# A second cross attention: query weights loaded first, the first batch's scores and softmax placed among the absorbed queries

## The chip, the cores and the metric

The kernel runs on one core of a Trainium2 chip. The metric is the device time of one execution in microseconds (us).

## What is computed

The reference is a perceiver-like network on `x` (8 batches x 64 tokens x 256 features) with a context of 8 x 1024 x 256: three sublayers (cross attention, a memory mixer, a mixture feed-forward), then three more, of which the first is the cross attention that the change touches. Each is added to the residual. Cut to that sublayer:

```python
x = x + _L1_xattn_ref(_layernorm(x), ctx_1024, ctx_1024, w_q, w_k, w_v, w_o)
# HEADS = 16, HEAD_DIM = 64, scale = HEAD_DIM ** -0.5
q = (query @ w_q).reshape(B, Q, HEADS, HEAD_DIM).transpose(0, 2, 1, 3)
k = (key @ w_k).reshape(B, Kl, HEADS, HEAD_DIM).transpose(0, 2, 1, 3)
v = (value @ w_v).reshape(B, Kl, HEADS, HEAD_DIM).transpose(0, 2, 1, 3)
scores = jnp.einsum('bhqd,bhkd->bhqk', q, k) * scale
attn = jax.nn.softmax(scores, axis=-1)
out = jnp.einsum('bhqk,bhkd->bhqd', attn, v)
return out.transpose(0, 2, 1, 3).reshape(B, Q, HEADS * HEAD_DIM) @ w_o
```

## The kernel before

The program runs the sublayers one after another, each as one or more blocks of five instruction streams (TensorE, VectorE, ScalarE, GpSimd, SyncE for the loads). A block ends for all engines together; inside it, the order of each engine's work is written out by hand and the engines wait for each other's semaphores. Precise products are made of three matmuls (`product3`) on a high half (a cast to fp32r) and a low half (value minus high half): high x high, high x low, low x high.

The second cross attention (`xattn1`, from line 1285) has three blocks.

Block e (lines 1314 to 1389). SyncE loads the key weights `wk` (L1327), the query weights `wq` (L1328), the context features of batch 0 (`rawT`, feature-major, L1307) and its keys (`raw`, L1310), 1 MB each. Meanwhile `Norm` normalises the residual and transposes it into `xnT`; it opens with 12 matmuls on the identity (L100). Both weights count on one semaphore, `w_in`, and ScalarE and TensorE wait for both loads. Then:

- Query projection, 8 groups p (two heads each): TensorE runs 4 matmul passes with `wq` (L1378) into one of two PSUM banks; ScalarE casts the result to `q_hi` (L1348), VectorE makes `q_lo` (L1363). In front, ScalarE casts all of `wk` (L1345) and GpSimd subtracts (L1335).
- Absorbed queries, 32 units u = (head, half of the 256 features): three matmuls with `wk` (64 rows each) into one of four PSUM banks; even units are evicted by ScalarE with the scale (L1351), odd ones by VectorE (L1367), into `e_qc`. After unit 0, ScalarE casts the context features, in two copies, to `e_cT_hi` (L1356).

Block f (from line 1395). It starts with the queries of batch 0 split into halves of four groups each: ScalarE casts 128x1024 (`f_qb_hi`, L1462), VectorE subtracts (L1529). GpSimd subtracts the features' high half in four pieces (`e_cT_lo`, L1436). TensorE then makes the scores of group 0 and group 1 (12 matmuls of 128x512 each, `scores`), which wait for all four pieces and for the first half of the queries. The softmax of a group p is: VectorE's maximum (L1541), ScalarE's exponential with the sum (L1474), VectorE's reciprocal and multiplication (L1547, L1549). After that the eight batches run, the first and last written out and the six between as a loop. In a batch TensorE transposes the probabilities of group p (L1594), makes the scores of group p + 2 and the outputs of an earlier pair of groups; ScalarE and VectorE split the transposed probabilities (L1482, L1536) and do the softmax of p + 2. In the last two groups the next batch's first two scores and the first softmax are made, so a batch starts with group 0 softmaxed and group 1 scored. SyncE loads the features and keys of the next batch as soon as the buffers have been read.

Block g multiplies by `w_v` and `w_o` and adds to the residual.

## Time and profile before

| | us |
|---|---|
| median of 3 runs | 1137.87 (1135.56 to 1143.01) |
| time of the profiled execution | 1139.35 |
| its span (first to last instruction) | 1137.6 |
| TensorE matmul busy | 1028.3 (90%) |
| VectorE busy | 559.2 (49%) |
| ScalarE busy | 494.1 (43%) |
| GpSimd busy | 209.5 (18%) |

One execution was profiled. Times in the profile are microseconds from the start of its span. PE is TensorE's matmuls, PEld its weight loads, DVE VectorE, ACT ScalarE, POOL GpSimd, SPq SyncE's DMA queue. A row of a timeline is one instruction or several alike in a row (x2, x8), written as output <- inputs with partitions x elements; its duration is that of the whole group, and overlapping matmuls have modelled ends, so their pace is read from the starts. The granted clock is a share of 2.4 GHz.

### The profile page before, as it was taken

To read this page: it belongs to the slowest core of one execution; us is meant where nothing else is said; L and a number is where in the kernel's file an instruction comes from. 1 tells how busy PE (TensorE), PEld (TensorE's weight loads), DVE (VectorE), ACT (ScalarE), POOL (GpSimd) and SP (SyncE) were. 2 spreads that over 40 slices of the span, in tenths; PEclk is the share of its full clock that TensorE was granted. 3 is DMA by queue.
4 is the path that set the end of the run, shared out by engine and by line. 5 is a ranking of instruction groups with operands and counts; after the bars stand their busy time and mean duration, and the time that the engine had idled before them with its cause. 6 is when DMAs were issued, how large, how long until landed. Compare 5 with 4: busy or idle time off the path is not lost. (4 is left out here: it accounts for less than half of the span.)

```text
span 1137.6 us, 20074 instructions
## 1 busy us (share of the span) xinstructions
PE 1028.3 (90%) x8322; PEld 863.3 (76%) x8322; DVE 559.2 (49%) x837; ACT 494.1 (43%) x719; POOL 209.5 (18%) x173
## 2 busy tenths in 40 slices
PE   8999999745779997879999999999999988969997
PEld 6787778515458995569898989898988956459997
DVE  3556655667744343554645454555465512373211
ACT  4566665331327662634444444444544411313222
POOL 2111120020603441131111111111303003120000
PEclk9899999987969998989999999999999999889999
DMA  4111110010112314020111111111030003912710
GB/s 135 60 58 41 44 42 2 6 37 16 44 38 66 94 62 148 1 75 13 63 37 37 37 37 37 37 37 37 37 111 0 1 1 111 380 43 90 243 39 19
DMA packets 49535, 68.75 MB, mean 60 GB/s; under 512 B 5744, under 2 KB 41024, under 8 KB 49472
## 3 DMA queue, kind: packets, MB, share of 16 engines
q1 hardware_dynamic: 49472, 67.83, 18.0%
q8 instruction: 49, 0.80, 0.3%
q14 instruction: 14, 0.11, 0.0%
HBM read 67.29 MB, written 0.52 MB: 60 GB/s over the span
## 5 line engine op out<-in xcount | busy, mean ns | idle before, releaser
L1474 ACT ACTIVATE f_pr<-ps,f_negmax 128x1024 f32<-128x1024 f32 x64 | 71.4, 1116 | 178.9 <-DVE f_negmax L1541 178.9
L181 PE MATMUL ps<-f_pT_hi,f_cN_hi 128*128 128x256 f32 x512 | 145.3, 284 | 2.4 <-DVE f_pT_lo L1536 2.4
L181 PE MATMUL ps<-f_pT_hi,f_cN_lo 128*128 128x256 f32 x512 | 144.8, 283 | 0.0
L181 PE MATMUL ps<-f_pT_lo,f_cN_hi 128*128 128x256 f32 x512 | 144.8, 283 | 0.0
L1536 DVE TENSOR_TENSOR f_pT_lo<-ps,f_pT_hi 128x1024 fp32r<-128x1024 f32 x64 | 78.2, 1222 | 78.6 <-ACT f_pT_hi L1482 78.6
L378 DVE SCALAR_TENSOR_TENSOR a_u<-ps,a_floor,a_cap 128x1024 f32<-128x1024 f32 x64 | 79.2, 1279 | 75.5 <-PE ps L468 75.5
L181 PE MATMUL ps<-e_cT_hi,f_qb_hi 128*128 128x512 f32 x256 | 106.2, 415 | 8.0 <-POOL e_cT_lo L1436 8.0
L181 PEld LDWEIGHTS ps<-f_pT_hi,f_cN_hi 128*128 128x128 f32 x512 | 98.0, 191 | 4.8 <-DVE f_pT_lo L1536 2.6
L181 PE MATMUL ps<-e_cT_hi,f_qb_lo 128*128 128x512 f32 x256 | 101.1, 395 | 0.0
L181 PE MATMUL ps<-e_cT_lo,f_qb_hi 128*128 128x512 f32 x256 | 100.5, 393 | 0.0
L181 PEld LDWEIGHTS ps<-f_pT_lo,f_cN_hi 128*128 128x128 f32 x512 | 98.0, 191 | 1.6
L181 PEld LDWEIGHTS ps<-f_pT_hi,f_cN_lo 128*128 128x128 f32 x512 | 98.0, 191 | 0.0
L318 ACT ACTIVATE a_pr<-a_u,a_nb 128x1024 f32<-128x1024 f32 x64 | 73.7, 1152 | 52.0 <-DVE a_u L378 50.7
L1541 DVE TENSOR_REDUCE f_negmax<-ps 128x1 f32<-128x1024 f32 x64 | 78.1, 1220 | 36.8 <-PE ps L181 36.8
L1482 ACT CAST f_pT_hi<-ps 128x1024 fp32r<-128x1024 f32 x64 | 64.9, 1014 | 53.9 <-PE ps L1594 53.9
L1436 POOL TENSOR_TENSOR e_cT_lo<-e_rawT,e_cT_hi 128x512 fp32r<-128x512 f32 x32 | 42.3, 1357 | 220.4 <-ACT e_cT_hi L1458 193.5
L1594 PE MATMUL ps<-ident,f_pr 128*128 128x128 f32 x512 | 66.6, 273 | 12.7 <-DVE f_pT_lo L1536 11.9
L1594 PEld LDWEIGHTS ps<-ident,f_pr 128*128 128x128 f32 x512 | 57.0, 140 | 17.8 <-issue 16.4
L100 PE MATMUL ps<-ident 128*128 128x128 f32 x240 | 37.6, 329 | 35.5 <-ACT b_cs L632 18.4
L1443 POOL TENSOR_TENSOR f_cN_lo<-e_raw,f_cN_hi 128x512 fp32r<-128x512 f32 x32 | 43.7, 1396 | 120.7 <-ACT f_cN_hi L1469 120.7
L100 PEld LDWEIGHTS ps<-ident 128*128 128x128 f32 x240 | 36.2, 243 | 38.1 <-ACT b_cs L632 19.2
L181 PEld LDWEIGHTS ps<-e_cT_hi,f_qb_hi 128*128 128x128 f32 x256 | 48.7, 190 | 16.4 <-POOL e_cT_lo L1436 8.4
(360 smaller groups left out, 2201.0 us busy)
## 6 DMA issues: line engine op xcount, KB each, us to landing
k_w<-in_L_ffn_W SPq DMA_DIRECT2D x22, 1024.0 KB, 9.8
a_ctxT<-in_ctxT SPq DMA_DIRECT2D x16, 512.0 KB, 4.4
d_w<-in_L_ffn_w SPq DMA_DIRECT2D x32, 256.0 KB, 2.8
e_rawT<-in_ctxT SPq DMA_DIRECT2D x8, 1024.0 KB, 4.9
e_raw<-in_ctx SPq DMA_DIRECT2D x8, 1024.0 KB, 5.3
e_wk<-in_L_xattn_w_k SPq DMA_DIRECT2D x1, 1024.0 KB, 7.1
e_wq<-in_L_xattn_w_q SPq DMA_DIRECT2D x1, 1024.0 KB, 9.2
g_wv<-in_L_xattn_w_v SPq DMA_DIRECT2D x1, 1024.0 KB, 8.0
```

The source lines that it names most:

```text
L100: self.nc.tensor.matmul(self.bank(bank)[:, 0:P], self.ident[:], self.ident[:], start=True, stop=True)
L181: last = nc.tensor.matmul(out, a[i], b[j], start=start and n == 0, stop=stop and n == 2, skip_group_check=skip)
L318: A.activation(pr[:, n % NP, :], u[:, n % NU, :], ACT.Square, bias=nb[:], scale=HD ** -0.5).then_inc(p_ready, 1)
L378: V.scalar_tensor_tensor(u[:, n % NU, :].rearrange("p (r w) -> p r w", r=RT), core.psum[:, 0:2048].rearrange("p (r w) -> p r w", r=RT)[:, ...
L1436: nc.gpsimd.tensor_tensor(cT[1][:, c, cols], rawT[:, c, cols], cT[0][:, c, cols].bitcast(F32), ALU.subtract).then_inc(t_lo, 1)
L1443: nc.gpsimd.tensor_tensor(cN[1][:, ks, :], raw[:, ks, :], cN[0][:, ks, :].bitcast(F32), ALU.subtract).then_inc(n_lo, 1)
L1474: nc.scalar.activation(pr[:, p % NPR, :], core.ps[p % 2][:], ACT.Exp, bias=negmax[:, p:p + 1], accum_out=total[:, p:p + 1]).then_inc(exp_r ...
L1482: nc.scalar.copy(pT[0][:, g, :, P * (p % 2):P * (p % 2) + P], core.ps[2][:].rearrange("p (k n) -> p k n", n=P)).then_inc(pT_hi, 1)
L1536: nc.vector.tensor_tensor(pT[1][:, g, :, cols], core.ps[2][:].rearrange("p (k n) -> p k n", n=P), pT[0][:, g, :, cols].bitcast(F32), ALU.s ...
L1541: nc.vector.tensor_reduce(negmax[:, p:p + 1], core.ps[p % 2][:], AX, ALU.max, negate=True).then_inc(max_ready, 1)
L1594: last = nc.tensor.transpose(core.ps[2][:, k * P:(k + 1) * P], pr[:, p % NPR, k * P:(k + 1) * P], core.ident[:])
```

## The change

The query weights are loaded first and have a semaphore of their own. The key weights' high and low halves are made in two pieces, and the features' high half in two, between the casts of the query projection (ScalarE after groups 0 and 1, and after 2 and 3); the low half of the features stands behind that of the key weights in GpSimd's queue, in block e. The units are evicted as before in two halves of 16; after each half, ScalarE waits until both engines' evictions are done and casts that half of batch 0's queries, and VectorE subtracts, in front of its next eviction. After unit 22 TensorE makes the scores of group 0; VectorE takes their maximum after evicting unit 23 and divides after evicting unit 29; ScalarE takes the exponential after evicting unit 26. After unit 31 TensorE makes the scores of group 1. Block f starts with the maximum of group 1 and then the batches, whose order stays. The buffers and helpers that both blocks now use are declared in front of them. No instruction is dropped; two are split in two (the key weights' cast and subtraction).

```diff
--- before.py
+++ after.py
@@ -1298,6 +1298,14 @@
+        NPR = 2
+        HALF = HP // 2
+        qb = [core.sb("e_qb_" + n, [P, DC, H * T], F32R, ctx) for n in ("hi", "lo")]
+        pr = core.sb("e_pr", [P, NPR, S], F32, ctx)
+        negmax, total = core.sb("e_negmax", [P, HP], F32, ctx), core.sb("e_total", [P, HP], F32, ctx)
+        qb_hi, qb_lo = core.sem("e_qb_hi"), core.sem("e_qb_lo")
+        s_psum, max_ready, exp_ready = core.sem("e_s_psum"), core.sem("e_max_ready"), core.sem("e_exp_ready")
+        recip, p_ready = core.sem("e_recip"), core.sem("e_p_ready")
         norm = Norm(core, "e")
...
@@ -1309,6 +1317,59 @@
         def load_keys(sp, b):
             sp.dma_start(raw[:], one(a["ctx"], b).rearrange("(k p) d -> p k d", p=P)).then_inc(n_in, 16)
 
+
+        def queries_of(b, half):
+            cols = slice(HALF * P * half, HALF * P * (half + 1))
+            return qc[:, :, b, cols] if isinstance(b, int) else \
+                qc[:, :, bass.ds(b, 1), cols].rearrange("p c o n -> p c (o n)")
+
+        def act_queries(b, half):
+            cols = slice(HALF * P * half, HALF * P * (half + 1))
+            nc.scalar.copy(qb[0][:, :, cols], queries_of(b, half)).then_inc(qb_hi, 1)
+
+        def dve_queries(dve, b, half):
+            cols = slice(HALF * P * half, HALF * P * (half + 1))
+            dve.wait_ge(qb_hi, 2 * b + half + 1)
+            nc.vector.tensor_tensor(qb[1][:, :, cols], queries_of(b, half), qb[0][:, :, cols].bitcast(F32),
+                                    ALU.subtract).then_inc(qb_lo, 1)
+
+        def pool_features(pool, b):
+            for i in range(4):
+                c, cols = i // 2, slice(S // 2 * (i % 2), S // 2 * (i % 2 + 1))
+                pool.wait_ge(t_hi, 2 * b + c + 1)
+                nc.gpsimd.tensor_tensor(cT[1][:, c, cols], rawT[:, c, cols], cT[0][:, c, cols].bitcast(F32),
+                                        ALU.subtract).then_inc(t_lo, 1)
+
+        def act_exponentials(act, b, p):
+            act.wait_ge(max_ready, HP * b + p + 1)
+            nc.scalar.activation(pr[:, p % NPR, :], core.ps[p % 2][:], ACT.Exp, bias=negmax[:, p:p + 1],
+                                 accum_out=total[:, p:p + 1]).then_inc(exp_ready, 1)
+
+        def dve_maximum(dve, b, p):
+            dve.wait_ge(s_psum, HP * b + p + 1)
+            nc.vector.tensor_reduce(negmax[:, p:p + 1], core.ps[p % 2][:], AX, ALU.max,
+                                    negate=True).then_inc(max_ready, 1)
+
+        def dve_divide(dve, b, p):
+            n = HP * b + p
+            dve.wait_ge(exp_ready, n + 1)
+            nc.vector.reciprocal(total[:, p:p + 1], total[:, p:p + 1]).then_inc(recip, 1)
+            dve.wait_ge(recip, n + 1)
+            nc.vector.tensor_scalar(pr[:, p % NPR, :], pr[:, p % NPR, :], total[:, p:p + 1], None,
+                                    ALU.mult).then_inc(p_ready, 1)
+
+        def pe_scores(pe, b, p):
+            if p == 0:
+                pe.wait_ge(t_lo, 4 * b + 4)
+            if p % HALF == 0:
+                pe.wait_ge(qb_lo, 2 * b + p // HALF + 1)
+            wait_if_positive(pe, exp_ready, HP * b + p - 1)
+            for h in range(2):
+                for c in range(DC):
+                    last = product3(nc, core.bank(2 * (p % 2) + h),
+                                    [q[:, c, p * P:(p + 1) * P] for q in qb],
+                                    [t[:, c, 512 * h:512 * h + 512] for t in cT], c == 0, c == DC - 1)
+            last.then_inc(s_psum, 1)
 
         with ExitStack() as inner:
             sb = lambda name, shape, dt=F32: core.sb("e_" + name, shape, dt, inner)
...
@@ -1316,23 +1377,28 @@
             q2 = [sb("q_" + n, [P, HP, NT], F32R) for n in ("hi", "lo")]
-            w_in, wk_hi, wk_lo = sem("w_in"), sem("wk_hi"), sem("wk_lo")
+            wq_in, wk_in, wk_hi, wk_lo = sem("wq_in"), sem("wk_in"), sem("wk_hi"), sem("wk_lo")
             q_psum, q_hi, q_lo = sem("q_psum"), sem("q_hi"), sem("q_lo")
             c_psum, c_act, c_dve, dve_step = sem("c_psum"), sem("c_act"), sem("c_dve"), sem("dve_step")
             block = inner.enter_context(nc.Block())
             NB = 4
+            EARLY = 22
 
             @block.sync
             def _(sp):
-                sp.dma_start(wk[:], a["L1_xattn_w_k"].rearrange("(p r) d -> r p d", r=P)).then_inc(w_in, 16)
-                sp.dma_start(wq[:], a["L1_xattn_w_q"].rearrange("(c p) o -> p c o", p=P)).then_inc(w_in, 16)
+                sp.dma_start(wq[:], a["L1_xattn_w_q"].rearrange("(c p) o -> p c o", p=P)).then_inc(wq_in, 16)
+                sp.dma_start(wk[:], a["L1_xattn_w_k"].rearrange("(p r) d -> r p d", r=P)).then_inc(wk_in, 16)
                 load_features(sp, 0)
                 load_keys(sp, 0)
 
             @block.gpsimd
             def _(pool):
-                pool.wait_ge(wk_hi, 1)
-                nc.gpsimd.tensor_tensor(wk2[1][:], wk[:], wk2[0][:].bitcast(F32), ALU.subtract).then_inc(wk_lo, 1)
+                for i in range(2):
+                    pool.wait_ge(wk_hi, i + 1)
+                    ps = slice(HALF * i, HALF * (i + 1))
+                    nc.gpsimd.tensor_tensor(wk2[1][:, ps, :], wk[:, ps, :], wk2[0][:, ps, :].bitcast(F32),
+                                            ALU.subtract).then_inc(wk_lo, 1)
+                pool_features(pool, 0)
 
             def into(u):
                 h, c = u // DC, u % DC
@@ -1340,20 +1406,33 @@
 
             @block.scalar
             def _(act):
-                norm.scalar(act)
-                act.wait_ge(w_in, 32)
-                nc.scalar.copy(wk2[0][:], wk[:]).then_inc(wk_hi, 1)
-                for p in range(HP):
+                def high(p):
                     act.wait_ge(q_psum, p + 1)
                     nc.scalar.copy(q2[0][:, p, :], core.bank(2 + p % 2)).then_inc(q_hi, 1)
-                for u in range(0, H * DC, 2):
+
+                def evict(u):
                     act.wait_ge(c_psum, u + 1)
                     nc.scalar.mul(into(u), core.bank(4 + u % NB).rearrange("p (b q) -> p b q", b=B),
                                   HD ** -0.5).then_inc(c_act, 1)
-                    if u == 0:
+
+                norm.scalar(act)
+                for p in range(HP):
+                    high(p)
+                    if p < 2:
+                        act.wait_ge(wk_in, 16)
+                        ps = slice(HALF * p, HALF * (p + 1))
+                        nc.scalar.copy(wk2[0][:, ps, :], wk[:, ps, :]).then_inc(wk_hi, 1)
+                    elif p < 4:
                         act.wait_ge(t_in, 16)
-                        for c in range(DC):
-                            nc.scalar.copy(cT[0][:, c, :], rawT[:, c, :]).then_inc(t_hi, 1)
+                        nc.scalar.copy(cT[0][:, p - 2, :], rawT[:, p - 2, :]).then_inc(t_hi, 1)
+                for half in range(2):
+                    for u in range(H * half, H * (half + 1), 2):
+                        evict(u)
+                        if u == EARLY + 4:
+                            act_exponentials(act, 0, 0)
+                    act.wait_ge(c_act, HP * (half + 1))
+                    act.wait_ge(c_dve, HP * (half + 1))
+                    act_queries(0, half)
 
             @block.vector
             def _(dve):
@@ -1362,15 +1441,31 @@
                     dve.wait_ge(q_hi, p + 1)
                     nc.vector.tensor_tensor(q2[1][:, p, :], core.bank(2 + p % 2), q2[0][:, p, :].bitcast(F32),
                                             ALU.subtract).then_inc(q_lo, 1)
-                for u in range(1, H * DC, 2):
-                    dve.wait_ge(c_psum, u + 1)
-                    nc.vector.tensor_scalar(into(u), core.bank(4 + u % NB).rearrange("p (b q) -> p b q", b=B),
-                                            HD ** -0.5, None, ALU.mult).then_inc(c_dve, 1)
+                for half in range(2):
+                    for u in range(H * half + 1, H * (half + 1), 2):
+                        dve.wait_ge(c_psum, u + 1)
+                        nc.vector.tensor_scalar(into(u), core.bank(4 + u % NB).rearrange("p (b q) -> p b q", b=B),
+                                                HD ** -0.5, None, ALU.mult).then_inc(c_dve, 1)
+                        if u == EARLY + 1:
+                            dve_maximum(dve, 0, 0)
+                        if u == EARLY + 7:
+                            dve_divide(dve, 0, 0)
+                    dve.wait_ge(c_dve, HP * (half + 1))
+                    dve_queries(dve, 0, half)
 
             @block.tensor
             def _(pe):
+                def unit(u):
+                    h, c = u // DC, u % DC
+                    pe.wait_ge(q_lo, h // 2 + 1)
+                    if u >= NB:
+                        pe.wait_ge(c_dve if u % 2 else c_act, (u - NB) // 2 + 1)
+                    rows = slice(HD * (h % 2), HD * (h % 2) + HD)
+                    product3(nc, core.bank(4 + u % NB), [w[rows, h // 2, c * P:(c + 1) * P] for w in wk2],
+                             [q[rows, h // 2, :] for q in q2], True, True).then_inc(c_psum, 1)
+
                 norm.tensor(pe)
-                pe.wait_ge(w_in, 32)
+                pe.wait_ge(wq_in, 16)
                 for p in range(HP):
                     if p >= 2:
                         pe.wait_ge(q_lo, p - 1)
@@ -1378,15 +1473,12 @@
                         last = nc.tensor.matmul(core.bank(2 + p % 2), wq[:, c, p * P:(p + 1) * P], xnT[:, c, :],
                                                 start=c == 0, stop=c == DC - 1)
                     last.then_inc(q_psum, 1)
-                pe.wait_ge(wk_lo, 1)
+                pe.wait_ge(wk_lo, 2)
                 for u in range(H * DC):
-                    h, c = u // DC, u % DC
-                    pe.wait_ge(q_lo, h // 2 + 1)
-                    if u >= NB:
-                        pe.wait_ge(c_dve if u % 2 else c_act, (u - NB) // 2 + 1)
-                    rows = slice(HD * (h % 2), HD * (h % 2) + HD)
-                    product3(nc, core.bank(4 + u % NB), [w[rows, h // 2, c * P:(c + 1) * P] for w in wk2],
-                             [q[rows, h // 2, :] for q in q2], True, True).then_inc(c_psum, 1)
+                    unit(u)
+                    if u == EARLY:
+                        pe_scores(pe, 0, 0)
+                pe_scores(pe, 0, 1)
 
...
@@ -1457,10 +1527,6 @@
...
@@ -1502,33 +1566,24 @@
...
-                queries(0, 0)
-                queries(0, 1)
-                exponentials(0, 0)
                 exponentials(0, 1)
                 each(act, B, batch)
 
...
-                queries(0, 0)
-                queries(0, 1)
-                maximum(0, 0)
-                divide(0, 0)
-                maximum(0, 1)
+                        dve_maximum(dve, b + 1, 0)
+                        dve_queries(dve, b + 1, 1)
+                        dve_divide(dve, b + 1, 0)
...
-                scores(0, 0)
-                scores(0, 1)
                 each(pe, B, batch)
```

## Rows read from the trace of the kernel before

**Rows 1.** Table by stages: stretch, busy us (instructions) per engine, granted clock, DMA share, GB/s.

```profile
442.30:446.50 4.20, 0.00 (x0) 0.00 (x0) 0.65 (x1) 0.57 (x2) 0.00 (x0) 1.00 1.02 411
446.50:450.40 3.90, 3.82 (x5) 1.63 (x6) 0.00 (x0) 2.30 (x2) 1.96 (x1) 0.56 0.84 277
450.40:462.00 11.60, 11.60 (x28) 4.77 (x26) 4.84 (x7) 3.67 (x7) 2.56 (x1) 1.00 0.01 2
479.00:486.70 7.70, 0.00 (x0) 0.00 (x0) 3.98 (x3) 3.27 (x3) 6.89 (x4) 0.64 0.01 2
486.70:491.20 4.50, 4.45 (x11) 3.49 (x12) 0.00 (x0) 0.00 (x0) 0.00 (x0) 0.50 0.64 233
...
500.00:900.00 400.00, 388.85 (x2619) 355.71 (x2620) 217.83 (x257) 186.29 (x254) 78.82 (x60) 1.00 0.12 40
```

**Rows 2.** Transfers issued 436 to 440: count, KB, us from issue to landing.

```profile
e_wk<-in_L_xattn_w_k SPq DMA_DIRECT2D x1, 1024.0 KB, 7.1
e_wq<-in_L_xattn_w_q SPq DMA_DIRECT2D x1, 1024.0 KB, 9.2
```

**Rows 3.** Timeline of SyncE's queue: start, us, engine, line, operation.

```profile
436.81 0.38 SPq L1327 DMA_DIRECT2D e_wk<-in_L_xattn_w_k  x1
437.24 0.58 SPq L1328 DMA_DIRECT2D e_wq<-in_L_xattn_w_q  x1
```

**Rows 4.** Timeline of TensorE, same columns; in brackets the idle time before and its releaser.

```profile
446.58 15.67 PE L1378 MATMUL ps<-xnT,e_wq 128*128 128x512 f32 x32 [4.36 <-DMA e_wq<-in_L_xattn_w_q]
462.18 0.49 PE L181 MATMUL ps<-e_q_hi,e_wk_hi 64*128 64x512 f32 x1
...
468.79 0.59 PE L181 MATMUL ps<-e_q_hi,e_wk_hi 64*128 64x512 f32 x2
...
477.83 0.46 PE L181 MATMUL ps<-e_q_hi,e_wk_hi 64*128 64x512 f32 x1
...
486.75 0.79 PE L181 MATMUL ps<-e_cT_hi,f_qb_hi 128*128 128x512 f32 x1 [7.98 <-POOL e_cT_lo L1436]
...
491.74 0.40 PE L181 MATMUL ps<-e_cT_hi,f_qb_hi 128*128 128x512 f32 x1
...
494.26 0.39 PE L181 MATMUL ps<-e_cT_hi,f_qb_lo 128*128 128x512 f32 x1
495.44 1.09 PE L1594 MATMUL ps<-ident,f_pr 128*128 128x128 f32 x8 [0.79 <-DVE f_pr L1549]
```

**Rows 5.** Timeline of VectorE.

```profile
478.81 0.69 DVE L1367 TENSOR_SCALAR e_qc<-ps 128x512 f32<-128x512 f32 x1 [0.29 <-PE ps L181]
480.87 3.48 DVE L1529 TENSOR_TENSOR f_qb_lo<-e_qc,f_qb_hi 128x1024 fp32r<-128x1024 f32 x2 [1.37 <-ACT f_qb_hi L1462]
...
494.63 0.75 DVE L1549 TENSOR_SCALAR f_pr<-f_pr,f_total 128x1024 f32<-128x1024 f32 x1
495.30 1.22 DVE L1541 TENSOR_REDUCE f_negmax<-ps 128x1 f32<-128x1024 f32 x1
...
526.07 1.23 DVE L1529 TENSOR_TENSOR f_qb_lo<-e_qc,f_qb_hi 128x1024 fp32r<-128x1024 f32 x1 [2.70 <-ACT f_qb_hi L1462]
```

**Rows 6.** Timeline of ScalarE; the first two rows are from the stage before.

```profile
340.97 1.28 ACT L923 ACT_TABLE_LOAD   x1 [2.82 <-PE ps L181]
342.26 0.69 ACT L923 ACTIVATE d_h<-ps,d_b 128x512 f32<-128x512 f32 x1
...
462.29 0.59 ACT L1348 CAST e_q_hi<-ps 128x512 fp32r<-128x512 f32 x1 [1.13 <-PE ps L1378]
...
463.67 1.98 ACT L1356 CAST e_cT_hi<-e_rawT 128x1024 fp32r<-128x1024 f32 x2
...
479.80 1.99 ACT L1462 CAST f_qb_hi<-e_qc 128x1024 fp32r<-128x1024 f32 x2 [1.26 <-PEq L1313]
...
493.20 1.12 ACT L1474 ACTIVATE f_pr<-ps,f_negmax 128x1024 f32<-128x1024 f32 x1 [10.11 <-DVE f_negmax L1541]
```

**Rows 7.** Timeline of GpSimd.

```profile
479.81 6.89 POOL L1436 TENSOR_TENSOR e_cT_lo<-e_rawT,e_cT_hi 128x512 fp32r<-128x512 f32 x4 [26.85 <-POOLq L1313]
```

79 lines of the change are left out of this document (13 added, 66 removed).

## The prediction

> **What bounds the kernel now.** I looked first at the table by stages. In 400 us of the batch loop of the second cross attention TensorE is busy 388.85 us and the other engines half of that or less [rows 1]: there the matmul stream sets the time, and the change touches nothing in it. The change lies in front of it, between 436.8 and 500 us, so I read that stretch from the transfers to the engines' timelines. Three places show TensorE waiting or slow:
>
> - 442.3 to 446.5: TensorE does nothing [rows 1]. It waits for the query weights: their load is issued second, at 437.24, and lands 9.2 us later, at 446.4; the key weights, issued at 436.81, land at 443.9 [rows 2, 3]. The matmuls start at 446.58 after 4.36 us idle [rows 4], and at 446.5 to 450.4 the granted clock is 0.56, so most of that stretch lies at 1.2 GHz; then it is 1.00 (2.4 GHz) [rows 1].
> - The 32 units that make the absorbed queries start at 462.18; the last starts at 477.83. From the twelfth unit (468.79) to the last they come every 9.04 / 20 = 0.452 us [rows 4]. All 31 steps at that pace would be 14.0 us, but take 15.65: 1.6 us are lost early, where ScalarE makes two copies of the context features (1.98 us at 463.67) between two evictions [rows 6].
> - From the last unit to the first score matmul TensorE is idle 7.98 us, until 486.75 [rows 4]: the block ends at 479.50 with VectorE's last eviction [rows 5], and only then are the queries split (ScalarE 479.80, VectorE 480.87) and the low half of the features made on GpSimd (6.89 us for four, from 479.81) [rows 5 to 7]. The scores start at 1.2 GHz (0.50 until 491.2 [rows 1]). VectorE reaches the second maximum at 495.30 [rows 5].
>
> A measurement of this kernel can tell about 1% (11.4 us) from no change. The profiled run has a span of 1137.6 us and took 1139.35; the median of the runs shown is 1137.87. I make the sum in the span and take it off the median.
>
> **The change part by part.** All times after are counted from U, the start of the first unit.
>
> *Query weights first.* If the first of the two loads lands where the first lands now, TensorE starts at 444.0 and not at 446.58: 2.55 us. Bounds: its own landing time, 9.2 us from an issue at 436.81, gives 446.0, a gain of 0.5; the other end is the transposed input, whose copy on VectorE ends at 442.95 (0.65 us of the stretch from 442.3 [rows 1]), a gain of 3.6. I take the landing of the first load, since it is the place in the queue that changes. The key weights then land at about 446.4. ScalarE needs them after the first query cast, at about 446.1 + 0.6, so they cost nothing; a microsecond of lateness would be hidden too, for two PSUM banks give TensorE one group (4 x 0.43 us) of slack.
>
> *Clock.* The idle time before these matmuls shrinks from 4.36 to about 1.8 us. The clock was still 1.00 through the idle stretch and fell just after it [rows 1]; before the gap of 0.79 us ahead of the first transposes no fall follows [rows 1, 4]. A gap of 1.8 us lies between 0.79 (no fall) and 4.36 (fall). I take no fall, since in the trace the clock held for the first 4 us of idleness. The 32 matmuls took 15.6 us to U; at full clock 32 x 0.43 = 13.8 and a tail of 0.1 give 13.9 (at full clock the 11.6 us from 450.4 hold 28 matmuls, so 27 steps of 0.43 [rows 1]; the four matmuls of a group take 1.72). That is 1.7 us; the bound on the other side is 0. So U moves from 462.18 to 457.9, by 4.25 us.
>
> *Feature and key-weight halves moved into the query projection.* ScalarE gets 0.95 to 1.04 us (half of the 1.98 [rows 6]) more in each of four groups of 1.72 us, beside a cast of 0.59 [rows 6]: 1.63, so it just keeps up, and TensorE hides it. Should the steps between engines push it over, each of the four groups would lose 0.2 us at most, 0.8 in all. GpSimd splits the key weights and then the features; by 6.89 us for the four from about 452.5 it is done at 459.4, and the first scores ask for them at U + 12.4 = 470.3: 11 us of cover. The units lose the stall of 1.6 us.
>
> *Units 0 to 15.* 32 units took 479.50 - 462.18 = 17.3 us to the last eviction; less the stall 15.7, less 16 x 0.452: the sixteenth is evicted at U + 8.5.
>
> *First half of the queries.* ScalarE copies 128x1024 (half of 1.99, 1.0 to 1.05), VectorE subtracts (1.23 when GpSimd is quiet, the row at 526.07 [rows 5]): U + 10.85. VectorE's next eviction (0.69), of unit 17, waits behind it: 11.6. Unit 21 needs that bank. TensorE would have reached unit 21 at about U + 9.7, so this new wait costs 1.8 us; units 21 and 22 end at 12.4.
>
> *First scores between units 22 and 23.* Twelve matmuls step by (494.26 - 491.74) / 11 = 0.229 us at full clock [rows 4]: 2.75 us, to U + 15.15. Queued behind them are units 23 to 31. Unit 23 is evicted 0.98 us after its start (477.83 to 478.81 [rows 4, 5]): 16.15 to 16.85. Behind it on VectorE stands the maximum, 1.22 [rows 5]: 18.1, then evictions 25 and 27 (18.8, 19.5), each 1.22 late. Unit 29 waits for eviction 25, so its own ends at 20.5.
>
> *First exponential.* ScalarE evicts units 24 and 26 by 17.8, then loads the exponential's table. The same load before Gelu took 1.28 us and the activation started 1.29 us after the load did [rows 6]: 19.1, a microsecond after the maximum. The exponential to the end of the division took 495.38 - 493.20 = 2.18 us [rows 5, 6], so the values are there at 21.3; with VectorE's eviction of 29 in front, 21.45. The Trainium skill says more against it: ScalarE: Activation LUTs, section "What ACT_TABLE_LOAD costs", gives about 1.38 us of drain besides the load, which would make this step 1.4 us later and the gain 11.1. The two rows of this trace leave no room for a drain, so the trace disagrees. In the old place the load was covered by the wait for the scores.
>
> *End of the block.* Eviction 31: 22.15. ScalarE copies the second half, 1.04: 23.2. VectorE subtracts, 1.23: 24.5. The second scores (12 matmuls) run beside this. The next block began 0.30 us after the last instruction of this one (479.50 to 479.80 [rows 5, 6]): VectorE takes the second maximum at U + 24.8. From there the old queue order holds: TensorE's transposes need its division and the low half in the same sequence. SyncE's loads of the next features and keys are only asked for earlier and had tens of microseconds of cover.
>
> *Sum.* Before, VectorE took the second maximum at 495.30 - 462.18 = 33.1 us after U; afterwards at 24.8. That is 8.3 us (1.6 of it the stall, 2.0 the score matmuls that ran at 1.2 GHz, 0.2 us each for the ten or so of the stretch at 0.50 [rows 1]). With the 4.25 before U: 12.5 us. Span 1137.6 to 1125.1; the median 1137.87 to 1125.4, or -1.1%.
>
> **The rivals.**
>
> - *The clock falls all the same* at the query projection: 1.7 us back, 1127.1. For it: the trace has no gap of this size. Against: the clock held for 4 us. 0.13.
> - *The query weights land no sooner than 446.0.* For it: they are a load of their own layout, and both share the same engines. Against: both move 1 MB in a stream of about 411 GB/s [rows 1]. 2.05 and with it the 1.7 of the clock are lost: gain 8.7, 1129.1. 0.1.
> - *The interleaving costs more than worked out.* Every wait in the chain from U + 8.5 to U + 24.8 crosses engines, and evictions, maximum, division and table load stand in two queues. One more eviction pair per engine late at both halves, or the table load paid a second time for the plain activations behind the exponential (1.28 each way), costs 1.5 to 4 us: gain 8.5 to 11, about 1128. Against a second load: none stands in front of the activations that run now under the square root's table. 0.18.
> - *Features not ready:* GpSimd's low half would have to come 11 us later than worked out. Then the scores wait inside the unit loop and take evictions with them; at 13 us late it gives 1127.5. 0.02.
> - *Slower:* VectorE and ScalarE enter the batch loop with the second softmax still to do, where now half of it is done, and never catch up, so that each of the 56 transposes after the first batch waits as the first does, 0.79 us [rows 4]. That is 44 us, or 1169; from 0.22 us each (12.5 / 56) the gain is gone. Against: TensorE is 97% busy there and a lag on two engines at half load is soon absorbed. 0.02.
>
> **How the numbers follow.** My forecast (gain 11 to 14) has 0.55, the rivals 0.13, 0.10, 0.18, 0.02 and 0.02. The likeliest is 1125.4 us. The low end adds the 1.1 us of the upper bound of the load, and 1.8 us if the new wait at unit 21 is covered: 1122.5. The high end takes in the late weights and most of the interleaving rival: 1130.5. Faster by over 1% is below 1126.5: most of the forecast's chance and a small part of the others, 0.51. Within 1%: 0.47. Slower: 0.02.
>
> **What the changed profile would show.** The query matmuls start at about 444.0 with a granted clock of 1.00 behind them; the first unit at about 457.9 and no ScalarE feature copy among the units; a break of 2 us around unit 21; twelve score matmuls 0.23 us apart from about 470; a table load between evictions 26 and 28; the next block at about 482.7, with TensorE idle some 2 us before it; the batches as long as before. The prediction is wrong if the first matmul starts past 445.5, if the clock is 0.5 behind it, or if that block starts after 485.

## The result, and the profile after

| | before | after |
|---|---|---|
| median, us | 1141.66 (5 runs) | 1130.53 (5 runs) |
| lowest to highest | 1135.56 to 1143.51 | 1125.99 to 1132.17 |
| span of the profiled execution | 1137.6 | 1130.5 |

The ratio is 0.9907, with a 95% interval of 0.9884 to 0.993: about 0.9% faster. The forecast was -1.1% (0.989) and 1125.4 us, and its range ended at 1130.5, 0.03 us short of the median. Two more runs moved the median of the kernel before from 1137.87, from which the forecast was taken off, to 1141.66.

Totals differ by 8 us from run to run, so I read the change in a stretch inside one trace: from the issue of the block's first load to VectorE's second maximum. Before, that is 436.81 [rows 3] to 495.30 [rows 5], 58.49 us. After, it is 441.99 to 487.96, 45.97 us: **12.52 us less, where the sum of the forecast had 12.5.** Both ends of this difference are single traces; what the others say stands below the table of experiments.

The loads of the changed kernel (columns as in [rows 2] and [rows 3]):

```profile
e_wq<-in_L_xattn_w_q SPq DMA_DIRECT2D x1, 1024.0 KB, 6.2
e_wk<-in_L_xattn_w_k SPq DMA_DIRECT2D x1, 1024.0 KB, 8.7
```

```profile
441.99 0.38 SPq L1389 DMA_DIRECT2D e_wq<-in_L_xattn_w_q  x1
```

TensorE's timeline, to be held against [rows 4]:

```profile
448.76 14.00 PE L1473 MATMUL ps<-xnT,e_wq 128*128 128x512 f32 x32 [0.79 <-DVE xnT L148]
462.69 0.50 PE L181 MATMUL ps<-e_q_hi,e_wk_hi 64*128 64x512 f32 x1
...
471.54 0.40 PE L181 MATMUL ps<-e_q_hi,e_wk_hi 64*128 64x512 f32 x1
...
473.11 0.47 PE L181 MATMUL ps<-e_q_hi,e_wk_hi 64*128 64x512 f32 x1 [0.71 <-ACT e_qc L1415]
...
474.55 0.59 PE L181 MATMUL ps<-e_q_hi,e_wk_hi 64*128 64x512 f32 x2 [0.51 <-DVE e_qc L1447]
...
475.53 0.50 PE L181 MATMUL ps<-e_cT_hi,e_qb_hi 128*128 128x512 f32 x1
```

and the end of the first scores, unit 23, and the batches' first transposes:

```profile
478.16 0.39 PE L181 MATMUL ps<-e_cT_hi,e_qb_lo 128*128 128x512 f32 x1
478.48 0.50 PE L181 MATMUL ps<-e_q_hi,e_wk_hi 64*128 64x512 f32 x2
...
487.96 1.06 PE L1619 MATMUL ps<-ident,e_pr 128*128 128x128 f32 x8 [1.22 <-PEq L1374]
```

Stages as in [rows 1]:

```profile
448.70:462.60 13.90, 13.84 (x32) 5.80 (x32) 4.85 (x8) 7.87 (x11) 9.60 (x6) 1.00 0.48 168
...
472.70:475.50 2.80, 1.88 (x9) 1.13 (x9) 2.30 (x3) 1.35 (x3) 0.00 (x0) 1.00 0.00 0
```

The query weights land at 441.99 + 6.2 = 448.2. The projection starts at 448.76, 6.77 us after the first issue (9.77 before), and runs wholly at 2.4 GHz: 13.93 us to the first unit, not 15.60. Before unit 20 (473.11) TensorE waits 0.71 us for ScalarE's eviction and before unit 21 (474.55) 0.51 us for VectorE's; units 19 and 20 stand alone, where the units around them come two by two. Then come the twelve score matmuls.

VectorE, against [rows 5]:

```profile
448.01 0.69 DVE L148 COPY xnT<-ps 128x512 f32<-128x512 f32 x1 [1.50 <-PE ps L171]
...
472.57 1.23 DVE L1333 TENSOR_TENSOR e_qb_lo<-e_qc,e_qb_hi 128x1024 fp32r<-128x1024 f32 x1 [1.25 <-ACT e_qb_hi L1328]
...
479.47 0.69 DVE L1447 TENSOR_SCALAR e_qc<-ps 128x512 f32<-128x512 f32 x1 [3.27 <-PE ps L181]
480.08 1.22 DVE L1350 TENSOR_REDUCE e_negmax<-ps 128x1 f32<-128x1024 f32 x1
...
483.00 0.69 DVE L1447 TENSOR_SCALAR e_qc<-ps 128x512 f32<-128x512 f32 x1 [0.52 <-PE ps L181]
...
483.80 0.75 DVE L1358 TENSOR_SCALAR e_pr<-e_pr,e_total 128x1024 f32<-128x1024 f32 x1
484.47 0.68 DVE L1447 TENSOR_SCALAR e_qc<-ps 128x512 f32<-128x512 f32 x1
486.40 1.23 DVE L1333 TENSOR_TENSOR e_qb_lo<-e_qc,e_qb_hi 128x1024 fp32r<-128x1024 f32 x1 [1.25 <-ACT e_qb_hi L1328]
487.96 1.23 DVE L1350 TENSOR_REDUCE e_negmax<-ps 128x1 f32<-128x1024 f32 x1 [0.33 <-PEq L1374]
```

ScalarE, against [rows 6]:

```profile
471.42 1.05 ACT L1328 CAST e_qb_hi<-e_qc 128x1024 fp32r<-128x1024 f32 x1 [0.88 <-DVE e_qc L1447]
...
480.85 1.28 ACT L1345 ACT_TABLE_LOAD   x1
482.14 1.12 ACT L1345 ACTIVATE e_pr<-ps,e_negmax 128x1024 f32<-128x1024 f32 x1
...
485.25 1.05 ACT L1328 CAST e_qb_hi<-e_qc 128x1024 fp32r<-128x1024 f32 x1 [0.93 <-DVE e_qc L1447]
```

The chain can be read off: copy of the first half at 471.42, subtraction 472.57, with the evictions of both engines behind them; after the scores the eviction of unit 23 (479.47), the maximum (480.08), the table load (480.85 to 482.13), the exponential, the eviction of unit 29 (483.00), the division (483.80), the eviction of unit 31 (484.47), copy and subtraction of the second half (485.25, 486.40), and the next block with the second maximum at 487.96.

### The profile page after: what moved, and what is told of

It is laid out like the page before. It is cut to its first block and busy times, and to the rows that moved or that the text cites. A ratio compares the mean times of both kernels' runs of the same rounds, so it can differ in the third digit from the quotient of the medians.

```text
span 1130.5 us, 20038 instructions
## 1 busy us (share of the span) xinstructions
PE 1028.9 (91%) x8322; PEld 866.3 (77%) x8322; DVE 557.4 (49%) x837; ACT 493.8 (44%) x720; POOL 207.6 (18%) x174
## 5 line engine op out<-in xcount | busy, mean ns | idle before, releaser
L1345 ACT ACTIVATE e_pr<-ps,e_negmax 128x1024 f32<-128x1024 f32 x64 | 71.4, 1115 | 170.5 <-DVE e_negmax L1350 164.3
L181 PE MATMUL ps<-e_cT_hi,e_qb_hi 128*128 128x512 f32 x256 | 105.4, 412 | 0.0
L181 PE MATMUL ps<-e_cT_hi,e_qb_lo 128*128 128x512 f32 x256 | 100.6, 393 | 0.0
L181 PE MATMUL ps<-e_cT_lo,e_qb_hi 128*128 128x512 f32 x256 | 99.9, 390 | 0.0
L1350 DVE TENSOR_REDUCE e_negmax<-ps 128x1 f32<-128x1024 f32 x64 | 78.1, 1220 | 30.4 <-PE ps L181 30.1
L1619 PE MATMUL ps<-ident,e_pr 128*128 128x128 f32 x512 | 66.5, 273 | 13.1 <-DVE f_pT_lo L1591 11.8
L1619 PEld LDWEIGHTS ps<-ident,e_pr 128*128 128x128 f32 x512 | 57.1, 140 | 18.1 <-issue 17.9
L286 POOL TENSOR_TENSOR a_ctx_lo<-a_ctxT,a_ctx_hi 128x1024 fp32r<-128x1024 f32 x14 | 33.3, 2404 | 136.6 <-ACT a_ctx_hi L298 136.6
```

Of the source, the lines that this page charges most:

```text
L181: last = nc.tensor.matmul(out, a[i], b[j], start=start and n == 0, stop=stop and n == 2, skip_group_check=skip)
L1345: nc.scalar.activation(pr[:, p % NPR, :], core.ps[p % 2][:], ACT.Exp, bias=negmax[:, p:p + 1], accum_out=total[:, p:p + 1]).then_inc(exp_r ...
L1350: nc.vector.tensor_reduce(negmax[:, p:p + 1], core.ps[p % 2][:], AX, ALU.max, negate=True).then_inc(max_ready, 1)
L1619: last = nc.tensor.transpose(core.ps[2][:, k * P:(k + 1) * P], pr[:, p % NPR, k * P:(k + 1) * P], core.ident[:])
```

## Where the rest of the 1,130 us went

The stretch gained 12.52 us, but the two spans differ by 7.1. The traces place the rest outside the stretch:

| part | before, us | after, us | difference |
|---|---|---|---|
| start to the block's first load | 436.81 | 441.99 | +5.18 |
| the stretch | 58.49 | 45.97 | -12.52 |
| second maximum to VectorE's first copy in block g | 431.63 | 433.44 | +1.81 |
| that copy to its first addition to the residual | 18.32 | 18.32 | 0.00 |
| from there to the last norm's statistics | 60.41 | 58.94 | -1.47 |
| the last sublayer | 131.94 | 131.84 | -0.10 |

The first line is the feed-forward sublayer in front, which the change leaves alone. In its first part TensorE is idle for a fifth of the time; before:

```profile
281.43:354.86 73.43, 58.99 (x406) 42.15 (x407) 41.58 (x70) 30.00 (x42) 24.44 (x18) 0.84 0.16 45
354.86:436.81 81.95, 78.68 (x504) 70.94 (x502) 34.48 (x61) 48.82 (x79) 32.33 (x25) 1.00 0.23 71
```

and after:

```profile
281.03:359.04 78.01, 63.59 (x406) 46.20 (x407) 41.45 (x70) 30.09 (x42) 24.42 (x18) 0.78 0.15 43
359.04:441.99 82.95, 79.68 (x504) 71.85 (x502) 34.49 (x61) 48.81 (x78) 32.29 (x25) 0.97 0.24 70
```

VectorE and ScalarE do the same work in both (41.58 and 41.45 us busy; 30.00 and 30.09), TensorE the same 406 matmuls in 4.6 us more, at a lower granted clock. Half-clock time is (1 - 0.84) x 2 x 73.43 = 23.5 us in the one and (1 - 0.78) x 2 x 78.01 = 34 in the other. The second part took 1.00 us more, at 0.97 instead of 1.00, and the stages in front of both 0.40 us less. I take none of this for a cost of the change: of the twelve traces of this study, four had 72.8 to 73.8 us here (granted clock 0.84: the kernel before and three variants of the changed kernel, with its buffers) and eight had 76.4 to 78.0 (0.78 to 0.80: three variants of the kernel before among them). The -1.47 us of the fifth line goes with the clock too: 0.86 granted before, 0.91 after, for the same matmuls.

The 1.81 us in the batches are two things. In the last batch TensorE waits for the last softmax; behind that stretch the clock fell in the changed kernel's trace

```profile
905.96:909.50 3.54, 1.18 (x11) 0.94 (x10) 1.23 (x1) 1.50 (x2) 0.00 (x0) 1.00 0.00 0
909.50:914.00 4.50, 4.50 (x27) 4.50 (x27) 0.00 (x0) 0.00 (x0) 0.00 (x0) 0.64 0.00 0
```

and not in that of the kernel before

```profile
913.30:917.30 4.00, 1.64 (x14) 1.40 (x13) 1.23 (x1) 1.50 (x2) 0.00 (x0) 1.00 0.00 0
917.30:921.30 4.00, 4.00 (x36) 4.00 (x35) 0.00 (x0) 0.00 (x0) 0.00 (x0) 1.00 0.00 0
```

which makes about 1.45 us. It too comes and goes: a variant of the kernel before had the fall, and of eight traces with the change's buffers two had none. Whether the change makes it more frequent, these counts do not show. The remaining 0.35 us is spread evenly over the first seven batches: they took 373.8 to 374.0 us in all eight traces of the changed kernel and its variants, and 373.5 us in all four of the kernel before and its variants. That comes with the change, then; its cause is open.

## Experiments

In each trace I measured: start of the query projection and of the first unit, both from the block's first issue; from the first unit to the second maximum; and the whole stretch.

| kernel | projection | first unit | unit to maximum | stretch |
|---|---|---|---|---|
| before | 9.77 | 25.37 | 33.12 | 58.49 |
| after | 6.77 | 20.70 | 25.27 | 45.97 |
| after_again | 6.79 | 20.72 | 25.25 | 45.97 |
| after_third | 7.53 | 21.46 | 26.83 | 48.29 |
| wq_first | 6.49 | 20.39 | 33.42 | 53.81 |
| warm_gap | 10.44 | 24.27 | 32.61 | 56.88 |
| features_early | 9.27 | 26.16 | 26.44 | 52.60 |
| scores_last | 6.49 | 20.39 | 24.13 | 44.52 |
| divide_last | 6.38 | 20.30 | 24.63 | 44.93 |
| table_early | 7.47 | 21.40 | 26.77 | 48.17 |
| table_again | 7.01 | 20.94 | 25.26 | 46.20 |
| combined | 6.81 | 20.74 | 22.41 | 43.15 |

Where the query weights are loaded first, the start of the projection varies by 1.1 us, with the clock granted from the first issue to that start: 6.38 us at 0.77, 7.53 us at 0.59. So early terms are read from the first two columns and late ones from "unit to maximum".

The kernel before has only one trace, and its loads were late in it: the key weights landed after 7.1 us and the query weights after 9.2, but in warm_gap and features_early, which keep its order of loads, after 6.5 and 8.6, and 6.6 and 8.7; the projection of features_early starts at 9.27. So about 0.5 us of the gain before the first unit, and of the 12.52, may be chance. The other way round, after_third has 48.29 and not 45.97. The mean of the three traces of the changed kernel is 46.7 us, 11.7 less than before.

**The change once more (after_again).** No edit.

> The changed kernel as it is, once more beside the kernel before. I measure two things in each trace: the stretch from the issue of the block's first load to VectorE's second maximum (58.49 us before, 45.97 after), and the time at which that block starts (436.81 before, 441.99 after, in code that the change doesn't touch). Theory: the change is worth 12.5 us in its own stretch, and what is missing in the medians (11.1) is spread of the unchanged stages. Then the stretch is again 46.0 within 0.6 us, the block's start lies elsewhere in 436 to 442, and the ratio over more rounds is 0.989 to 0.991. Rival: the moved buffers or the blocks ahead are slower for good; then the block starts at 441 to 443 again.

Measured: stretch 45.97; the block started at 438.37, between the two earlier values; median 1130.38 us of 6 runs against 1139.28 of 11, ratio 0.992 (0.9895 to 0.9945). The stretch repeats to the hundredth, and the block's start does not. The rival falls. The ratio of 0.992 lies just outside the expected 0.989 to 0.991, on the weak side, and the stretch alone (12.5 / 1140 = 1.1%) is more than either comparison gives (0.9% and 0.8%): something in some runs takes part of it back (see after_third).

**Only the loads and the key weights' halves (wq_first).** To the kernel before (shortened; GpSimd's subtraction is split in two as well):

```diff
-sp.dma_start(wk...).then_inc(w_in, 16)
-sp.dma_start(wq...).then_inc(w_in, 16)
+sp.dma_start(wq...).then_inc(wq_in, 16)
+sp.dma_start(wk...).then_inc(wk_in, 16)
...
+for p in range(HP):            # ScalarE
+    (cast of q, group p)
+    if p < 2: wait wk_in; cast half p of wk
```

> The kernel before with the query weights loaded first and the key weights' halves made in two pieces among the query casts; the features and the scores stay where they were. Theory: the first unit starts 20.7 us after the block's first issue, as in the changed kernel (25.4 before): 3.0 us from the earlier start of the query projection, 1.7 from the clock that stays at 2.4 GHz. The stretch to the second maximum is 58.5 - 4.7 = 53.8 us. Rival (the load order is worth nothing alone, since the key weights now come late): 56 to 58.5.

Measured: first unit at 20.39, stretch 53.81. TensorE's projection in this trace:

```profile
448.09 13.97 PE L1383 MATMUL ps<-xnT,e_wq 128*128 128x512 f32 x32 [1.29 <-DMA e_wq<-in_L_xattn_w_q]
```

13.97 us for the 32 matmuls, against 15.67 in [rows 4]. The two terms before the first unit are there without the rest of the change. That the stretch hits the expected 53.8 is partly luck: the first unit came 0.3 us sooner than expected, and from there to the maximum it took 0.3 us more than before.

**Only the clock (warm_gap).** To the kernel before:

```diff
 norm.tensor(pe)
+core.warm(7, 16)
 pe.wait_ge(w_in, 32)
```

> The kernel before with 16 more identity matmuls on TensorE where it waits for the query weights; nothing else changes. This measures the clock's term alone: the start of the query projection stays at +9.8 us from the block's first load. Theory: the clock stays at 2.4 GHz, the projection takes 13.9 us and not 15.6, and the stretch is 58.5 - 1.7 = 56.8 us. Rival (the clock falls for another reason than idleness): 58.5.

Measured, TensorE's timeline:

```profile
446.87 3.84 PE L100 MATMUL ps<-ident 128*128 128x128 f32 x32 [0.78 <-DVE xnT L148]
450.55 13.90 PE L1379 MATMUL ps<-xnT,e_wq 128*128 128x512 f32 x32
```

With the wait filled, the projection took 13.90 us (13.83 to the first unit): the clock's term is 15.60 - 13.83 = 1.77 us, though the query weights are still loaded second. The sixteen matmuls (two records each in the trace, like the twelve of the norm) ran until the projection's start and were a few too many: it began at 10.44, not 9.77. So the stretch, 56.88, hits the expected 56.8 by chance: 0.67 lost there, and about 0.5 won later, where fewer of the score matmuls ran at 1.2 GHz (eight of their steps took 0.4 us or more, and ten before).

**Only the features (features_early).** The edit, to the kernel before: ScalarE's two feature copies behind the casts of groups 2 and 3, GpSimd's four subtractions behind the key weights'; block f otherwise as before.

> The kernel before with only the features' halves moved: high half among the query casts, low half behind the key weights' on GpSimd, in the first block. Scores and softmax stay in the second. Theory: the units lose the stall of 1.6 us and the scores wait only for the first queries' low half (about 482.1 instead of 486.75), so the stretch is 58.5 - 1.6 - 4.6 = 52.3 us, or 50.3 if the clock stays up in the shorter idle time. Rival (it is the interleaving among the units that brings the gain): only the 1.6, 56.9.

Measured: 52.60. From the first unit to the maximum it is 26.44, 6.7 us less than before (expected 6.2). The projection started 0.5 us sooner than before, but took 1.3 us more to the first unit (16.89 and not 15.60), because more of it ran at 1.2 GHz:

```profile
449.10:455.20 6.10, 6.06 (x7) 2.50 (x8) 0.69 (x1) 2.41 (x2) 4.20 (x1) 0.50 0.64 216
486.00:490.00 4.00, 4.00 (x12) 3.10 (x11) 0.90 (x1) 0.00 (x0) 0.00 (x0) 0.59 0.13 51
```

The second row lies in the scores: they too still run in part at 1.2 GHz. So earlier features alone make 6.7 of the change's 7.85 us behind the first unit. The move of scores and softmax into block e adds 1.2 to that. The clock alone is about as much: the twelve score matmuls of group 0, on which the first maximum waits, took 3.78 us from the first start to the last here and 2.63 in the changed kernel. So the move in its interleaved form seems to have won little but the clock.

**Scores behind the last unit (scores_last).** To the changed kernel (shortened, with the softmax's lines in words):

```diff
 for u in range(H * DC):
     unit(u)
-    if u == EARLY:
-        pe_scores(pe, 0, 0)
+pe_scores(pe, 0, 0)
 pe_scores(pe, 0, 1)
...
-(maximum after unit 23, exponential after 26, division after 29)
+(all three behind the second half of the queries)
```

> The changed kernel with the scores of group 0 after the last unit instead of between units 22 and 23, and its maximum, exponential and division at the ends of the queues of VectorE and ScalarE. By the changed kernel's trace the interleaved maximum and division stand in front of VectorE's evictions, and so of the units and of the second half of the queries. Theory A: without them the last eviction is at about U + 17.4, the maximum runs behind the second half of the queries at U + 19.7, the division ends at U + 23.1, and the second maximum is at U + 23.5 against 25.3: stretch 44.2 us. Theory B (the interleaving hides the 2.75 us of score matmuls, as it is meant to): 47 to 49 us.

Measured: 24.13 from the first unit (23.5 expected; VectorE's last eviction already ends at U + 17.97 and not at U + 17.4, with U the start of the first unit), stretch 44.52: theory A. VectorE's timeline:

```profile
474.89 1.23 DVE L1333 TENSOR_TENSOR e_qb_lo<-e_qc,e_qb_hi 128x1024 fp32r<-128x1024 f32 x1 [1.25 <-ACT e_qb_hi L1328]
476.04 1.22 DVE L1350 TENSOR_REDUCE e_negmax<-ps 128x1 f32<-128x1024 f32 x1
...
479.80 1.23 DVE L1350 TENSOR_REDUCE e_negmax<-ps 128x1 f32<-128x1024 f32 x1 [0.33 <-PEq L1374]
```

The maximum starts straight behind the second half's subtraction, when the score matmuls have already run beside that subtraction and the last evictions. The interleaving costs 25.27 - 24.13 = 1.1 us rather than winning 2.75. By the two traces, it puts the maximum and the division in front of VectorE's last evictions, on which the end of the block hangs, while the score matmuls that it hides have cover in either place.

**Division last (divide_last).** In the changed kernel, `if u == EARLY + 7` became `if u == H * DC - 1`.

> The changed kernel with VectorE's division of group 0 behind its last eviction (unit 31) instead of behind unit 29. Theory: in the changed kernel's tail the division (0.94 us) stands in front of the last eviction, and so of ScalarE's copy and VectorE's subtraction of the second half of the queries; moved back it runs beside ScalarE's copy. The last eviction can start once unit 31 is there, 0.5 us earlier: stretch 45.4 us, bounds 45.0 and 45.97. Rival: the block's end is held by the second scores on TensorE: 45.9.

Measured: 24.63, so 0.64 us less than the 25.27 of the changed kernel; the expected 45.4 is 0.57 less. (The stretch, 44.93, lies just under the expected lower bound of 45.0: the projection started 0.4 us earlier here.) VectorE:

```profile
477.15 1.51 DVE L1447 TENSOR_SCALAR e_qc<-ps 128x512 f32<-128x512 f32 x2 [0.51 <-PE ps L181]
...
478.77 0.75 DVE L1358 TENSOR_SCALAR e_pr<-e_pr,e_total 128x1024 f32<-128x1024 f32 x1
479.92 1.22 DVE L1333 TENSOR_TENSOR e_qb_lo<-e_qc,e_qb_hi 128x1024 fp32r<-128x1024 f32 x1 [0.40 <-ACT e_qb_hi L1328]
481.48 1.23 DVE L1350 TENSOR_REDUCE e_negmax<-ps 128x1 f32<-128x1024 f32 x1 [0.33 <-PEq L1374]
```

The division now runs beside ScalarE's copy, and the subtraction (479.92) waits only 0.40 us for it, not 1.25. The rival, that the second scores hold the block's end, falls.

**Table loaded early (table_early, table_again).** In the changed kernel, behind the norm on ScalarE:

```diff
 norm.scalar(act)
+act.wait_ge(norm.xnT, DC)
+nc.scalar.activation(core.std[:, 0:1], core.vareps[:, 0:1], ACT.Exp, scale=-1.0)
```

> The changed kernel with an exponential of one column of 128 values behind the norm on ScalarE, so that the table's load happens there and not in front of the first exponential. The prediction held the load (1.28 us, of it 0.84 past the maximum) for part of the chain, together with VectorE's eviction of unit 29. Theory: the eviction alone carries it, and the stretch stays at 46.0 within 0.2. Rival: the load is on the chain: 45.1; a drain of 1.4 us besides the load would make it less still.

Measured: stretch 48.17, worse than either theory, and 26.77 from the first unit. ScalarE:

```profile
443.79 1.28 ACT L1420 ACT_TABLE_LOAD   x1
...
478.01 1.11 ACT L1345 ACTIVATE e_pr<-ps,e_negmax 128x1024 f32<-128x1024 f32 x1 [0.51 <-DVE e_negmax L1350]
```

The exponential now starts right behind the maximum, but the clock had fallen at unit 21. Past that, from the last score matmul of group 0 (474.85) to the second maximum (484.64), it takes 9.79 us; in the changed kernel 487.96 - 478.16 = 9.80. So it wins nothing that the load is gone from there. The changed kernel's trace agrees: VectorE's eviction of unit 29 ends at 483.69, and ScalarE is done with the exponential at 483.34. Whether the early load had anything to do with the fall was asked once more:

> The kernel with the table's early load once more. In its first trace the clock fell to 1.2 GHz for 3.4 us between units 21 and the first scores, right behind TensorE's two waits there (0.71 and 0.51 us), which two traces of the changed kernel had without a fall. Theory: the fall is a matter of when in time the two waits lie, and not of the early load. Then the first unit to the second maximum takes either 25.3 us (no fall) or about 26.8 (fall), and the clock shows which; 25.3 is the likelier. Rival (the extra instruction on ScalarE causes it): 26.8 again.

Measured: 25.26 from the first unit, no fall. So the early load does not bring the fall each time; and without a fall, the part takes the same with the load in front of the exponential (25.27 and 25.25 in the changed kernel) as without it: the load costs nothing. And the changed kernel itself:

> The changed kernel a third time, for the same question and for the spread of the unchanged stages. Theory: first unit to second maximum 25.3 us, or 26.8 if the clock falls at unit 21; the stage between 281 and 355 us, which the change doesn't touch, takes either 73 to 74 us (granted clock 0.84) or 76.5 to 78 (0.78), as in all ten traces so far. Rival (the moved buffers make that stage slower): always the longer one; but two variants with the same buffers had the shorter one, so I expect either.

Measured: 26.83 from the first unit, with the fall. TensorE's timeline and the stages in this trace:

```profile
471.32 0.47 PE L181 MATMUL ps<-e_q_hi,e_wk_hi 64*128 64x512 f32 x1 [0.71 <-ACT e_qc L1415]
...
472.76 0.89 PE L181 MATMUL ps<-e_q_hi,e_wk_hi 64*128 64x512 f32 x2 [0.52 <-DVE e_qc L1447]
...
474.43 0.79 PE L181 MATMUL ps<-e_cT_hi,e_qb_hi 128*128 128x512 f32 x1
```

```profile
472.70:476.10 3.40, 3.34 (x10) 2.43 (x11) 1.21 (x2) 0.78 (x2) 0.00 (x0) 0.53 0.02 5
476.10:487.00 10.90, 9.57 (x48) 6.52 (x47) 5.95 (x9) 5.72 (x8) 0.00 (x0) 0.99 0.00 0
```

The waits of 0.71 and 0.52 us are those of the first trace, but at 472.7 the clock goes to 1.2 GHz until 476.1 and the pair of units and the first scores run at half pace. That is 26.83 - 25.27 = 1.56 us. Of the six traces in which the scores stand between the units, two had it and four had not; scores_last has the same two waits (0.70 and 0.52 us), without a fall. Each trace is one execution, so the share is rough. What decides it is not shown. The Trainium skill, TensorE: Matmul & The Clock Gate, section "A second HAM failure mode: psum-queue depth-cycling", says of another kernel, in bf16, that short idle times between groups of matmuls that cycle through PSUM banks made the clock go down and up again. These two traces look the same (0.53 granted in after_third), and the others show that here it does not happen each time.

The stage from 281 us took 76.6 us (granted clock 0.79 to 0.80): the long mode, which by itself says nothing against the rival; the short ones of scores_last, divide_last and table_early, with the same buffers, do.

**Both repairs (combined).** To scores_last (shortened):

```diff
+# GpSimd, behind the features
+pool.wait_ge(qb_hi, 1)
+nc.gpsimd.tensor_tensor(qb[1] first half, qc, qb[0], ALU.subtract).then_inc(qb_lo, 1)
...
 # ScalarE
 evict(u)
+if u == 20: wait for both engines' first 16 evictions; act_queries(0, 0)
-(the same after unit 14, and VectorE's dve_queries(0, 0))
```

> The kernel with the scores last (stretch 44.5 us), and in it the low half of the first queries on GpSimd instead of VectorE, asked for after ScalarE's eviction of unit 20, where its wait for both engines' first sixteen evictions is long over. Theory: the stall of 1.8 us at unit 21 (TensorE waiting behind VectorE's subtraction) shrinks to 0.5, the block's end and the second maximum move by 1.2 to 1.5: stretch 43.1 us, 15.4 less than before and 2.9 less than the changed kernel. Over rounds the ratio to the kernel before is 0.985 to 0.989. Rival: GpSimd's subtraction is so slow that the first scores wait for it: 44.5 or more.

Measured: 22.41 from the first unit, stretch 43.15, median 1125.96 us of 4 runs against 1142.24 of 7, ratio 0.9861 (0.9833 to 0.9889). VectorE and GpSimd:

```profile
478.02 1.23 DVE L1333 TENSOR_TENSOR e_qb_lo<-e_qc,e_qb_hi 128x1024 fp32r<-128x1024 f32 x1 [1.28 <-ACT e_qb_hi L1328]
479.17 1.22 DVE L1350 TENSOR_REDUCE e_negmax<-ps 128x1 f32<-128x1024 f32 x1
...
482.94 1.23 DVE L1350 TENSOR_REDUCE e_negmax<-ps 128x1 f32<-128x1024 f32 x1 [0.33 <-PEq L1374]
```

```profile
472.02 2.39 POOL L1404 TENSOR_TENSOR e_qb_lo<-e_qc,e_qb_hi 128x1024 fp32r<-128x1024 f32 x1 [12.20 <-ACT e_qb_hi L1328]
```

GpSimd needs 2.39 us for what VectorE did in 1.23, but nobody waits for it: it ends at 474.41, and the first scores, behind the last unit, start at 475.94, 15.41 us after the first unit (17.17 in scores_last). The stall at unit 21 is gone. In the stretch this version beats both kernels: 15.3 us less than before, 2.8 less than the changed one. Beside the kernel before, its total is 1.4% lower; beside the changed one it was not timed.

## Why the prediction was right and wrong

In order of its steps, counted from the first unit (U) where it did so:

| step | predicted | measured | difference |
|---|---|---|---|
| earlier projection | 2.55 | 3.00 | +0.45 |
| clock in the projection | 1.7 | 1.67 (warm_gap: 1.77) | 0 |
| first scores start | U + 12.4 | U + 12.84 | 0.44 late |
| unit 23 starts | U + 15.15 | U + 15.79 | 0.64 late |
| division ends | U + 21.45 | U + 21.86 | 0.41 late |
| second maximum | U + 24.8 | U + 25.27 | 0.47 late |
| the stretch | 12.5 less | 12.52 less | 0 |

That the last row agrees so closely is luck: 0.45 us won too much before the first unit and 0.47 us lost behind it cancel, the loads of the trace before were about 0.5 us late, and the clock did not fall at unit 21 in this trace. The mechanism is right, term by term, to about half a microsecond.

- **Query weights first: right, with another bound.** The first of the two loads landed after 6.2 us and not 7.1, and then it was no longer the load that TensorE waited for but VectorE's copy of the transposed input (448.01 + 0.69 = 448.70, projection at 448.76). The term is 3.0 us in place of 2.55; about 0.5 us of it may be the late loads of the one trace before.
- **Clock: right.** The gap shrank to 0.79 us; warm_gap shows the term by itself.
- **Stall at unit 21: right in kind, 0.44 us short.** The lateness builds up in small steps between the engines: ScalarE's copy starts at U + 8.73 (predicted 8.5), VectorE's subtraction ends at U + 11.11 (10.85), unit 21 starts at U + 11.86 (about 11.5), and units 21 and 22 take 0.98 us to the first score matmul and not 0.90. I had not seen that unit 20 waits too, 0.71 us for ScalarE's eviction, but unit 21 waits for VectorE behind it, so that cost nothing.
- **Table load: right, it costs nothing.** The sum had the exponential's path and the eviction of unit 29 within 0.2 us of each other and let the later win, the eviction; so it is in the trace, by 0.35 us, and table_again shows it by taking the load away. On the drain: the two rows of the prediction left ScalarE idle for 2.82 us in front of the load, where a drain could have hidden. In the changed kernel's trace ScalarE's eviction ends at 480.83, the load starts at 480.85, and the exponential starts at 482.14, 0.01 us after its end, so this trace disagrees with the 1.38 us of the Trainium skill (ScalarE: Activation LUTs, "What ACT_TABLE_LOAD costs").
- **A term was missing: the clock behind the new wait.** The prediction asked for the clock only where idle time shrank. At unit 21 the change makes new, short idle times, and in two of six traces the clock fell there, for 1.5 us. If a third of the executions have it, that is 0.5 us on the mean (an estimate from six traces). A fall at the end of the last batch costs as much again; whether the change adds to those, the traces do not show.
- **The baseline, and so the range: wrong.** This is the step that failed. The forecast took 12.5 us off a median of three runs, 1137.87, whose own range was 1135.56 to 1143.01; five runs gave 1141.66. Against that the same sum gives 1129.2, and the range 1126.3 to 1134.3 would have held 1130.53. The range was built from the terms of the change alone. The runs' spread of 8 us, for which the granted clock in unchanged stages accounts by up to 5 us in the traces, had no term in it. Five runs are few too: over all 24 runs of the kernel before in this study the median is 1140.1, over all 12 of the changed one 1130.6. By these the forecast time was 5.2 us too low, 2.3 of it the baseline and the rest the gain, 9.5 us and not 12.5.
- **Between 12.5 and the 9 to 11 of the medians** (11.13 and 8.90 us in the two comparisons) stay 1.4 to 3.6 us that I can only place in part: 0.35 in the batches in every trace, 0.5 on the mean at unit 21, about 0.5 for the late loads of the trace before, and the fall in the last batch, seen in six of eight traces with the change and in one of four without. Why the batches take 0.35 us more is open.
- **The rivals.** "The clock falls all the same" and "the weights land no sooner" did not come. "Interleaving costs more than worked out" came in small, 0.5 us, and 2.0 us in all in a trace with a fall at unit 21; against scores put last, the interleaving itself cost 1.1. The rival on the other side, a lag through all batches, did not appear: a batch is 0.05 us longer, not the 6.3 us (eight waits of 0.79) of that rival.

## What to carry to other kernels

Work moved into a stage pays by what it stops waiting for, not by being interleaved: making the features early was worth 6.7 us, loading in the order of need 4.7 (with the clock that this kept up, and perhaps 0.5 us of chance), and the interleaving of scores and units cost 1.1 against simply putting them last, because the short operations that it queued ahead of the evictions were on the chain and the matmuls that it hid were not. Where a total varies by more than the change is worth, measure between two fixed instructions of one trace, and let the range of a forecast carry the spread of the baseline as well as that of its terms.

## What the runs showed of the hardware that I had not expected

- The granted clock fell behind two waits of 0.71 and 0.51 us between short groups of matmuls, in two of six traces of one order; it stayed at 1.00 through a wait of 4.2 us before the projection in the kernel before and fell just after it.
- A stage that the change doesn't touch took 73 or 77 us by the clock it was granted (0.84 or 0.78). These 5 us are the largest part of the spread between the traces.
- The first load of a block of four, 1 MB, landed after 6.2 to 6.4 us in the nine traces with the query weights first, and after 6.5, 6.6 and 7.1 in the three with the key weights first; the second landed after 8.7 to 8.8, and 8.6, 8.7 and 9.2.
- GpSimd's subtraction of the features took 4.96 us for four where nothing else with two SBUF inputs ran on VectorE, against 6.89 beside VectorE's subtraction of the queries in [rows 7]. It was 4.94 to 4.97 in all nine traces of the first kind and 6.89 in all three of the second; VectorE's subtraction took 1.74 us each in the second kind, not 1.23.
